# Ranking edges on one Trainium2 core: histogram matmuls written out at fixed places, and a quarter of the one-hot tiles made by ScalarE

## The chip, the cores and the metric

The kernel runs on one core of one Trainium2 chip, as one launch. The metric is device time in microseconds (us), the median of the runs shown. A core has TensorE (PE in the profile; its weight loads are PEld), VectorE (DVE), ScalarE (ACT), GpSimd (POOL) and SyncE (SP), which only issues transfers. A "q" behind an engine's name is its sequencer.

## What is computed

The reference is a four-layer graph network on 3125 nodes with 256 features and 50000 edges. Each layer adds a graph part, a linear-attention part and a feed-forward or expert part to x. The graph parts gather by `src` and sum by `dst` (or the reverse), for instance in layer 1:

```
s = einsum('edh,edh->eh', q[row], k[col])
m = segment_max(s, row);  e = exp(s - m[row])
attn = e / segment_sum(e, row)[row]
out = segment_sum(attn[:, None, :] * v[col], row)
```

To do such sums tile by tile the kernel first sorts the edges. Nothing else of the reference matters here: the change touches only the sorting.

## The kernel before

The first stage, `rank_edges`, computes for each edge the place that it takes in a table sorted by its key, in two orders: order 0 by `dst`, order 1 by `src`. The 50000 edges lie in a [128, ET] layout with ET = 400 columns, of 125 partitions in use. A key is split into a high part (`hi_f`, which of NT = 25 blocks of 128 nodes) and a low part (`lo_f`, 0 to 127). A column of 128 edges is called a tile. The constants are SU = 16 tiles in a group and SB = 8 tiles in a batch, so an order has 25 groups and 50 batches.

In an order:

- VectorE (lines 239 to 242) casts and splits the keys and signals `cast`. TensorE transposes them (lines 365 and 366), ScalarE copies the rows out (lines 439 and 440), SyncE stores them in HBM and reads them back as broadcasts for each batch (line 227).
- VectorE then loops over the 25 groups. Line 246 makes the one-hot rows of the high parts of 16 tiles at once (`hot_hi`, 16x25 columns), line 249 makes those of the low parts (`hot_lo`), 16 instructions of 128x128 bf16, one for each tile. Each group raises `hot` by two.
- TensorE loops over the same groups (line 370). For each tile it waits for `hot`, loads `hot_lo` as weights and multiplies `hot_hi` (line 373), adding up a 128x25 histogram in PSUM. The place of each tile is computed from the loop's counter in registers. Line 376 closes the sum and raises `histogram`.
- Meanwhile VectorE fills the records that will be scattered (lines 253 to 261) and does the first comparisons of the first batch (lines 280 and 274). Line 274 needs ScalarE's first distance (line 447), eight Abs over the broadcast keys.
- VectorE waits for `histogram`, copies it (line 285), and a short chain between VectorE and TensorE (lines 287 to 304, 379, 380, 395, 425) makes the places at which the buckets begin.
- The ranking loop goes over the 50 batches: TensorE counts (lines 386 and 395) and chooses (lines 406 and 408), ScalarE copies (line 454) and takes distances (line 447), VectorE compares (lines 268 and 274), selects (lines 314 to 318) and, after each second batch, writes the addresses of 16 tiles (line 334), which raises `placed`.

GpSimd waits for the records of order 0, and then for `placed` of order 0 before each 16 tiles; it scatters each tile's records into a table in HBM by an indirect transfer (line 482, 400 of them). It does nothing for order 1 in this stage: those records are scattered in layer 1, beside other work. Order 1 starts on VectorE when order 0's addresses are all written. The stage ends when all engines are through, the scatters have landed and the stage's 53 semaphores are cleared; then `prepare` reads the sorted table back (line 522).

The same way of making a one-hot tile on ScalarE that the change uses stands in the edge stages of the layers: eight Abs of iota minus the low part, then one Relu of one minus that over all eight (lines 657 and 661, and 1568 and 1572).

Of the kernel before, what the change touches and what calls it, by code (L numbers as in the profile page):

```python
# [22 lines left out]
ACT = mybir.ActivationFunctionType  # L23
# [3 lines left out]
ds = bass.ds  # L27
# [3 lines left out]
NT = -(-N // P)  # L31
# [7 lines left out]
SU = 16  # L39
ET = -(-E // (125 * SU)) * SU  # L40
# [80 lines left out]
    return ap.unsqueeze(at).to_broadcast(shape)  # L121


def rank_edges(kit, name, orders, room):

    nc, dram = kit.nc, kit.dram
    assert EFULL * ET == E and ET % SU == 0 and SU == 2 * SB
    chunks = [(c, min(P, ET - c)) for c in range(0, ET, P)]
    BATCHES = ET // SB
    with Stage(kit, name) as s:  # L130
# [7 lines left out]
        lo_f = s.sb("lo_f", [P, ET])  # L138
        etype = s.sb("etype", [P, ET], I32)
        spill = s.sb("spill", [P, ET])  # L140
        hot_lo = s.sb("hot_lo", [P, ET, P], BF16)
        hot_hi = flat_xn.bitcast(BF16)[:, 0:ET * NT].rearrange("p (t b) -> p t b", t=ET)
# [36 lines left out]
        cast, hot, histogram, totals, prefix, based, begins = ({} for _ in range(7))  # L179
        rowed, rows_copied, rows_stored, distanced, equalled, spread = ({} for _ in range(6))  # L180
        counted, high, split, chosen, selected, placed, recorded = ({} for _ in range(7))
        for o in range(2):
            for at_, what in ((cast, "cast"), (hot, "hot"), (histogram, "histogram"), (totals, "totals"),
                              (prefix, "prefix"), (based, "based"), (begins, "begins"), (rowed, "rowed"),
                              (rows_copied, "rows_copied"), (rows_stored, "rows_stored"), (distanced, "distanced"),
                              (equalled, "equalled"), (spread, "spread"), (counted, "counted"), (high, "high"),
                              (split, "split"), (chosen, "chosen"), (selected, "selected"), (placed, "placed"),
                              (recorded, "recorded")):
                at_[o] = s.sem(f"{what}{o}")
# [9 lines left out]
        with nc.Block() as block:  # L199
# [33 lines left out]
            def _(dve):  # L233
# [3 lines left out]
                def order(o, q):  # L237
# [7 lines left out]
                    with dve.Fori(0, ET // SU) as i:  # L245
                        v.tensor_tensor(hot_hi[:, ds(i * SU, SU), :], bcast(hi_f[:, ds(i * SU, SU)], NT, 2),
                                        bcast(kit.iota[:, 0:NT], SU, 1), ALU.is_equal).then_inc(hot[o], 1)
                        for u in range(SU):
                            ins = v.tensor_scalar(hot_lo[:, ds(i * SU + u, 1), :].squeeze(1), iota_b[:],
                                                  lo_f[:, ds(i * SU + u, 1)], None, ALU.is_equal)  # L250
                        ins.then_inc(hot[o], 1)
# [108 lines left out]
            def _(pe):  # L360
                def order(o):
# [5 lines left out]
                    ins.then_inc(rowed[o], 1)  # L367

                    nc.tensor.matmul(ps_run[:, 0:NT], zero_b[:], zero_b[:, 0:NT], start=True, stop=True)
                    with pe.Fori(0, ET // SU) as i:  # L370
                        for u in range(SU):
                            pe.wait_ge(hot[o], i * 2 + 2)
                            nc.tensor.matmul(ps_run[:, 0:NT], hot_lo[:, ds(i * SU + u, 1), :].squeeze(1),
                                             hot_hi[:, ds(i * SU + u, 1), :].squeeze(1), start=False, stop=True,
                                             skip_group_check=True)
                    nc.tensor.matmul(ps_run[:, 0:NT], zero_b[:], zero_b[:, 0:NT], start=False, stop=True,
                                     skip_group_check=True).then_inc(histogram[o], 1)
                    pe.wait_ge(totals[o], 1)
# [53 lines left out]
            @block.scalar  # L432
            def _(act):
                def order(o):
                    act.wait_ge(rowed[o], 1)
                    if o:
                        act.wait_ge(rows_stored[0], 2 * 16 * len(chunks))
                    for j, (c, w) in enumerate(chunks):
                        nc.scalar.copy(key_row[0:w, j, :], ps_row[0:w, 0, j, :]).then_inc(rows_copied[o], 1)
                        nc.scalar.copy(lo_row[0:w, j, :], ps_row[0:w, 1, j, :]).then_inc(rows_copied[o], 1)  # L440

                    def distance(n, u):

                        act.wait_ge(lined[o][u], (n - u) * 16 + 32)
                        act.wait_ge(chosen[o], n + 1)
                        for k in range(SB):
                            ins = nc.scalar.activation(apart[:, u, k, :], key_line[:, u, k * P:(k + 1) * P], ACT.Abs,
                                                       scale=-1.0, bias=key_f[:, ds(n * SB + k, 1)])
                        ins.then_inc(distanced[o], 1)

                    def turn(n, u, more):
                        act.wait_ge(counted[o], n + 1)
                        act.wait_ge(chosen[o], n + 1)
                        nc.scalar.copy(parts[:, u, 0].rearrange("p k b -> p (k b)"),
                                       ps_count[:, u, 0:(SB + 1) * NT]).then_inc(high[o], 1)
                        if more:
                            distance(n + 1, 1 - u)

                    distance(0, 0)
                    pairs(act, turn)  # L460

                order(0)
                order(1)

            @block.gpsimd
# [3229 lines left out]
```

## Time and profile before

| what | value |
|---|---|
| median of 3 runs | 7550.93 us (7548.48 to 7556.42) |
| the profiled execution, its own time | 7552.14 us |
| its span, first to last instruction | 7550.2 us |
| TensorE busy | 5770.7 us (76%), 22573 matmuls |
| VectorE busy | 4088.7 us (54%) |
| ScalarE busy | 2739.3 us (36%) |
| GpSimd busy | 3202.7 us (42%) |
| mean granted TensorE clock | 0.838 |

Busy times are sums over the whole span; the ranking stage is its first tenth (0 to 722.9 us), so shares over the span say little of it. All times of the timeline count from the span's start. In a timeline a row gives start, length, engine, line, operation, output and input, and in brackets the idle time of the engine before it with what ended it. "x16" means that 16 instructions are merged in the row; its length goes from the first's start to the last's end, and neighbours overlap.

### The profile page before, as it was taken

The numbers are of one execution on the slowest core, as the hardware profiler recorded it, in microseconds if no ns is written. First come the engines' busy times: TensorE is split into PE (matmuls) and PEld (weight loads), VectorE is DVE, ScalarE is ACT, GpSimd is POOL, SyncE is SP. The second block draws the span as 40 slices with busy tenths as digits, with TensorE's granted clock in tenths as the row PEclk, the third lists the DMA queues.
The fourth block names the chain that finished last, engine by engine and source line by source line (L and its number), as shares of the span: only waits on it lengthen the run. The fifth ranks groups of instructions, "written<-read, shape, count | busy, mean of one in ns | idle before, by whom it ended". The sixth has DMA issues, their size and how long they took to land. (4 is left out here: it accounts for less than half of the span.)

```text
span 7550.2 us, 91454 instructions
## 1 busy us (share of the span) xinstructions
PE 5770.7 (76%) x22573; PEld 3591.7 (48%) x22664; DVE 4088.7 (54%) x9995; ACT 2739.3 (36%) x7575; POOL 3202.7 (42%) x3209
## 2 busy tenths in 40 slices
PE   5564688888985788876976787998788858998386
PEld 3332355554542565642545553554455535565253
DVE  7876577733113899966245334213577775556401
ACT  2524477721220444410114432113166615555010
POOL 1776576404772666610017750000177715553101
PEclk9999788888997778778988887898778766987597
DMA  2534222100001655510013330000144423333222
GB/s 87 165 86 155 50 50 47 31 12 28 2 2 53 172 158 157 159 32 13 0 60 105 105 75 23 0 0 14 47 117 115 112 58 105 98 98 69 76 99 74
DMA packets 268803, 549.15 MB, mean 73 GB/s; under 512 B 86992, under 2 KB 136588, under 8 KB 263692
## 3 DMA queue, kind: packets, MB, share of 16 engines
q0 software_dynamic: 134496, 314.63, 16.6%
q1 hardware_dynamic: 133932, 230.20, 9.5%
q8 instruction: 153, 2.51, 0.1%
q14 instruction: 222, 1.82, 0.1%
HBM read 495.56 MB, written 49.00 MB: 72 GB/s over the span
## 5 line engine op out<-in xcount | busy, mean ns | idle before, releaser
L1252 POOL DMA_INDIRECT L_edges_rows<-scratch_L_kv,L_edges_index x416 | 496.8, 1194 | 379.7 <-PE L_edges_ps_sum L1501 213.0
L1252 POOL DMA_INDIRECT L3a_edges_rows<-scratch_L3a,L3a_edges_index x416 | 462.5, 1112 | 409.5 <-DMA L3a_edges_last<-order_dst_last 257.1
L1252 POOL DMA_INDIRECT L3b_edges_rows<-scratch_L3b,L3b_edges_index x416 | 398.6, 958 | 400.8 <-PE L3b_edges_ps_sum L1501 236.3
L1702 POOL TENSOR_TENSOR L_norm_fold<-L_norm_square 128x400 f32<-128x400 f32 x64 | 66.6, 1040 | 1168.3 <-ACT L_norm_square L1711 1168.3
L482 POOL DMA_INDIRECT scratch_by_dst<-dst_record,dst_dest x400 | 439.7, 1099 | 271.1 <-DVE dst_dest L334 149.5
L1252 POOL DMA_INDIRECT L_edges_rows<-scratch_L,L_edges_index x416 | 424.4, 1020 | 257.3 <-issue 117.8
L632 POOL DMA_INDIRECT L_edges_rows<-scratch_L,L_edges_index x416 | 396.8, 954 | 274.5 <-SPq L616 148.0
L2324 DVE TENSOR_TENSOR L_experts_gated_h<-L_experts_hidden,L_experts_ps_g 128x800 f32<-128x800 f32 x112 | 110.6, 988 | 665.0 <-PE L_experts_ps_g L2277 665.0
L482 POOL DMA_INDIRECT scratch_by_src<-src_record,src_dest x400 | 383.1, 958 | 124.0 <-issue 121.7
L2315 ACT ACTIVATE L_experts_hidden<-L_experts_ps_h,L_eb_sb 128x400 f32<-128x400 f32 x320 | 190.2, 594 | 646.2 <-PE L_experts_ps_h L2270 646.2
L1373 DVE TENSOR_TENSOR L_acc<-L_edges_ps_sum,L_acc 128x264 f32 (+1 forms) x832 | 357.0, 429 | 98.5 <-DVE L_acc L1373 70.2
L644 PE MATMUL L_edges_ps_sum<-L_edges_rows,L_edges_hot 128*128 128x256 f32 x832 | 259.2, 476 | 143.8 <-issue 91.9
L684 DVE TENSOR_TENSOR L_acc<-L_edges_ps_sum,L_acc 128x256 f32 x416 | 176.7, 425 | 282.2 <-PE L_edges_ps_sum L644 248.2
L1501 PE MATMUL L3b_edges_ps_sum<-L3b_edges_rows,L3b_edges_hot 128*128 128x258 f32 x832 | 322.4, 536 | 4.2 <-DVE L_acc L1373 4.2
L2270 PE MATMUL L_experts_ps_h<-xn,L_e_sb 128*128 128x400 f32 x896 | 323.3, 504 | 2.6 <-PEq L113 2.6
L2287 PE MATMUL L_experts_ps_o<-L_experts_gated_h,L_e_sb 128*128 128x400 f32 x896 | 322.0, 499 | 2.2 <-DVE L_experts_gated_h L2324 2.2
L1501 PE MATMUL L_edges_ps_sum<-L_edges_rows,L_edges_hot 128*128 128x272 f32 x832 | 307.9, 503 | 6.1 <-DVE L_edges_rows L1355 6.1
L1568 ACT ACTIVATE L_edges_hot<-iota,L_edges_lo 128x128 f32<-128x128 f32 x832 | 252.8, 386 | 150.1 <-DMA L_edges_last<-order_src_last 92.8
L1604 ACT ACTIVATE L_edges_rhs<-L_edges_msg,L_edges_rhs 128x64 f32<-128x64 f32 x1248 | 303.6, 334 | 1.7
L1446 PE MATMUL L_edges_ps_key<-L_q,L_edges_hot_t 128*128 x832 | 270.5, 483 | 42.6 <-ACT L_edges_asked L1579 26.7
L1501 PE MATMUL L_edges_ps_sum<-L_edges_rhs,L_edges_hot 128*128 128x264 f32 x832 | 298.2, 491 | 0.0
L1501 PE MATMUL L3a_edges_ps_sum<-L3a_edges_rows,L3a_edges_hot 128*128 128x264 f32 x832 | 296.1, 488 | 0.6 <-issue 0.4
(767 smaller groups left out, 13541.3 us busy)
## 6 DMA issues: line engine op xcount, KB each, us to landing
x<-scratch_dst_key_rows SPq DMA_DIRECT2D x50, 512.0 KB, 4.7
x<-scratch_src_key_rows SPq DMA_DIRECT2D x50, 512.0 KB
L_experts_w<-in_L_w SPq DMA_DIRECT2D x16, 1024.0 KB
L_edges_rows<-scratch_L,L_edges_index POOLq DMA_INDIRECT x832
L_edges_lo_rows<-order_src_lo_rows SPq DMA_DIRECT2D x52, 256.0 KB
L3a_edges_lo_rows<-order_dst_lo_rows SPq DMA_DIRECT2D x52, 256.0 KB
L3b_edges_lo_rows<-order_dst_lo_rows SPq DMA_DIRECT2D x52, 256.0 KB
x<-scratch_dst_lo_rows SPq DMA_DIRECT2D x50, 256.0 KB, 3.7
```

The lines of the kernel that those rows point to most:

```text
L482: pool.indirect_dma_start(order["table"], bass.IndirectOffsetOnAxis(order["dest"][:, t:t + 1], 0), order["record"][:, t, :], None).then_in ...
L632: pool.indirect_dma_start(rows[:, n % RING, k, :], None, row_table, bass.IndirectOffsetOnAxis(index[:, t:t + 1].bitcast(U32), 0)).then_inc ...
L644: nc.tensor.matmul(ps_sum[:, k % 4, 0:F], hot[:, n % RING, k, :], rows[:, n % RING, k, :], start=True, stop=True).then_inc(summed, 1)
L1252: pool.indirect_dma_start(rows[:, n % RING, k, 0:RW], None, row_table, bass.IndirectOffsetOnAxis(index[:, t:t + 1].bitcast(U32), 0)).then_ ...
L1373: v.tensor_tensor(a, ps_sum[:, (c * SB + k) % BANKS, 0:M], a, ALU.add).then_inc(merged, 1)
L1446: ins = nc.tensor.matmul(ps_key[:, j % 2, (k % 2) * D:(k % 2 + 1) * D], hot_t[:, c % 2, k * P:(k + 1) * P], key_rows[:, ds(r[k], 1), :].sq ...
L1501: nc.tensor.matmul(ps_sum[:, (c * SB + k) % BANKS, 0:M], hot[:, c % RING, k, :], values(c)[:, k, :], start=True, stop=True).then_inc(summe ...
L1568: ins = nc.scalar.activation(hot[:, c % RING, k, :], kit.iota[:], ACT.Abs, scale=-1.0, bias=lo[:, ds(n * SB + k, 1)])
L1604: ins = nc.scalar.activation(out, src, ACT.Copy, scale=parts(c)[:, k, h, V:V + 1])
L2270: ins = nc.tensor.matmul(ps_h[:, (a + o) % 4, 0:CW], weights[l][:, e, f, o * P:(o + 1) * P], r, start=f == 0, stop=f == len(src) - 1)
L2287: nc.tensor.matmul(ps_o[:, o, 0:CW], weights[hid][:, e, f, o * P:(o + 1) * P], gated_h[:, n % 2, f, :], start=e == 0 and f == 0, stop=False)
L2315: nc.scalar.activation(hidden[l][:, n % 2, o, :], ps_h[:, a % 4, 0:CW], func, bias=biases[l][:, n % EX, o:o + 1]).then_inc(taken, 1)
```

## The change

Two edits, in both orders. VectorE's inner loop makes 12 of a group's 16 `hot_lo` tiles; ScalarE makes the last 4, between its copies of the rows and its first distance: four Abs of iota minus the low part into the tile's place, a wait for itself (`hot_apart`), and one Relu over the four tiles in place, which raises `hot_act`. In order 1 ScalarE first waits until TensorE has done all 50 counts of order 0, the last reads of the old tiles. TensorE's loop over groups is written out in the program: each tile has a fixed place, there is one wait for `hot` per group, and one for `hot_act` before the thirteenth tile. Four semaphores are new.

```diff
+ACT_TILES = 4
...
                     with dve.Fori(0, ET // SU) as i:
...
-                        for u in range(SU):
+                        for u in range(SU - ACT_TILES):
                             ins = v.tensor_scalar(hot_lo[:, ds(i * SU + u, 1), :].squeeze(1), iota_b[:],
                                                   lo_f[:, ds(i * SU + u, 1)], None, ALU.is_equal)
                         ins.then_inc(hot[o], 1)
...
-                    with pe.Fori(0, ET // SU) as i:
+                    for i in range(ET // SU):
+                        pe.wait_ge(hot[o], i * 2 + 2)
                         for u in range(SU):
-                            pe.wait_ge(hot[o], i * 2 + 2)
-                            nc.tensor.matmul(ps_run[:, 0:NT], hot_lo[:, ds(i * SU + u, 1), :].squeeze(1),
-                                             hot_hi[:, ds(i * SU + u, 1), :].squeeze(1), start=False, stop=True,
-                                             skip_group_check=True)
+                            if u == SU - ACT_TILES:
+                                pe.wait_ge(hot_act[o], i + 1)
+                            nc.tensor.matmul(ps_run[:, 0:NT], hot_lo[:, i * SU + u, :], hot_hi[:, i * SU + u, :],
+                                             start=False, stop=True, skip_group_check=True)
...
+                    act.wait_ge(cast[o], 1)
+                    if o:
+                        act.wait_ge(counted[0], BATCHES)
+                    for i in range(ET // SU):
+                        for u in range(SU - ACT_TILES, SU):
+                            ins = nc.scalar.activation(hot_lo[:, ds(i * SU + u, 1), :].squeeze(1), kit.iota[:], ACT.Abs,
+                                                       scale=-1.0, bias=lo_f[:, ds(i * SU + u, 1)])
+                        ins.then_inc(hot_apart[o], 1)
+                        act.wait_ge(hot_apart[o], i + 1)
+                        here = hot_lo[:, ds(i * SU + SU - ACT_TILES, ACT_TILES), :]
+                        nc.scalar.activation(here, here, ACT.Relu, scale=-1.0, bias=kit.ones[:, 0:1]).then_inc(hot_act[o], 1)
```

## Rows read from the trace of the kernel before

**Rows 1.** Stretches: us, busy (count) of PE, PEld, DVE, ACT, POOL, clock, DMA share, GB/s

```profile
19.00:103.50 84.50, 54.36 (x298) 31.57 (x298) 79.47 (x425) 3.80 (x16) 0.00 (x0) 1.00 0.12 39
...
475.50:700.30 224.80, 127.21 (x1306) 84.85 (x1306) 192.60 (x461) 137.01 (x442) 176.32 (x160) 1.00 0.56 168
```

**Rows 2.** Line 482, GpSimd's scatters: durations min/median/max, first and last start; what its idle time ended on

```profile
L482 POOL DMA_INDIRECT scratch_by_dst<-dst_record,dst_dest x400: 954/958/1992, 149.9 to 710.3; - x134
...
  DVE dst_dest L334: 149.5, 1
```

**Rows 3.** Timeline at the end of the ranking stage

```profile
700.06 0.18 DVE L334 TENSOR_TENSOR src_dest<-x,rank_spill 128x16 uint32<-128x16 f32 x1
...
710.33 0.95 POOL L482 DMA_INDIRECT scratch_by_dst<-dst_record,dst_dest  x1 [0.30 <-issue]
722.88 0.32 SPq L522 DMA_DIRECT2D prepare_dst_rec<-scratch_by_dst  x1
```

**Rows 4.** Timeline of order 0, from the histogram's groups to the ranking

```profile
26.47 0.57 DVE L246 TENSOR_TENSOR xn<-rank_hi_f,iota 128x400 f32 x1 [0.19 <-issue]
...
26.96 2.69 DVE L249 TENSOR_SCALAR rank_hot_lo<-rank_iota_b,rank_lo_f 128x128 bf16 x16
...
100.25 0.58 DVE L246 TENSOR_TENSOR xn<-rank_hi_f,iota 128x400 f32 x1 [0.17 <-issue]
...
110.05 1.22 DVE L274 SCALAR_TENSOR_TENSOR rank_apart<-rank_apart,rank_later_b 128x1024 bf16<-128x1024 bf16 x1
110.17 0.32 SPq L227 DMA_DIRECT2D x<-scratch_dst_lo_rows  x1
...
134.35 0.18 DVE L285 COPY rank_total<-rank_ps_run 128x25 f32<-128x25 f32 x1 [23.08 <-PE rank_ps_run L376]
...
142.36 2.44 ACT L447 ACTIVATE rank_apart<-x,rank_key_f 128x128 bf16<-128x128 f32 x8 [0.29 <-PE rank_ps_pick L408]
```

**Rows 5.** Timeline, TensorE, one group of the histogram in order 0

```profile
76.48 3.92 PE L373 MATMUL rank_ps_run<-xn,rank_hot_lo 128*128 x16 [0.54 <-issue]
```

**Rows 6.** Line 373: the register operations of TensorE's sequencer

```profile
L373 PEldq FUSED_REGOPS  x800: 74/74/89, 22.5 to 474.8; - x160
L373 PEldq ALU_OP  x800: 32/32/42, 22.7 to 474.9; - x160
```

**Rows 7.** Timeline, the first and the last of 16 choosing matmuls

```profile
141.49 0.21 PE L406 MATMUL rank_ps_pick<-rank_ones_b,rank_apart 128*128 128x1 bf16 x1
...
142.02 0.20 PE L408 MATMUL rank_ps_pick<-rank_parts,xn 128*128 128x50 bf16 x1
```

**Rows 8.** Groups by line, 19 to 104 us: busy us, mean ns, idle before

```profile
L249 DVE TENSOR_SCALAR rank_hot_lo<-rank_iota_b,rank_lo_f 128x128 bf16 x400 | 67.2, 249 | 0.0
```

**Rows 9.** Timeline, ScalarE: the last copy of rows, and eight Abs in layer 2

```profile
22.17 0.25 ACT L440 CAST rank_lo_row<-rank_ps_row 16x128 bf16<-16x128 f32 x1
...
3943.62 2.43 ACT L657 ACTIVATE L_edges_hot<-iota,L_edges_lo 128x128 f32<-128x128 f32 x8
```

**Rows 10.** Groups by line, ScalarE, whole span

```profile
L1568 ACT ACTIVATE L_edges_hot<-iota,L_edges_lo 128x128 f32<-128x128 f32 x832 | 252.8, 386 | 150.1 <-DMA L_edges_last<-order_src_last 92.8 <-DMA L_edges_dirs<-order_dst_dirs 57.3
...
L1572 ACT ACTIVATE L_edges_hot<-L_edges_hot,ones 128x1024 f32<-128x1024 f32 x104 | 119.4, 1148 | 3.4
...
L1713 ACT ACT_TABLE_LOAD x8 | 10.3, 1283 | 0.1
```

**Rows 11.** Transfers up to 160 us: issues, KB each, median us to landing

```profile
x<-scratch_dst_key_rows SPq DMA_DIRECT2D x8, 512.0 KB, 5.5
```

**Rows 12.** Timeline, order 1: VectorE's wait for the histogram

```profile
475.49 0.18 DVE L285 COPY rank_total<-rank_ps_run 128x25 f32<-128x25 f32 x1 [31.70 <-PE rank_ps_run L376]
```

**Rows 13.** Granted clock: mean of the core; then one stretch, columns as in rows 1

```profile
core 0: 7550.2 us, clock 0.838
...
7050.00:7144.00 94.00, 51.63 (x193) 37.49 (x192) 40.48 (x103) 7.93 (x10) 6.22 (x6) 0.57 0.19 77
```

**Rows 14.** Stretch from the histogram's copy to the first scatter, columns as in rows 1

```profile
134.35:149.90 15.55, 10.34 (x77) 6.51 (x78) 10.72 (x33) 7.84 (x26) 0.00 (x0) 1.00 0.34 103
```

More of the change, by code:

```diff
@@ L181, in rank_edges @@
         counted, high, split, chosen, selected, placed, recorded = ({} for _ in range(7))
+        hot_apart, hot_act = {}, {}
         for o in range(2):
-            for at_, what in ((cast, "cast"), (hot, "hot"), (histogram, "histogram"), (totals, "totals"),
+            for at_, what in ((cast, "cast"), (hot, "hot"), (hot_apart, "hot_apart"), (hot_act, "hot_act"), (histogram, "histogram"), (totals, "totals"),
                               (prefix, "prefix"), (based, "based"), (begins, "begins"), (rowed, "rowed"),
```

## The prediction

> **What bounds the kernel now.** Only the ranking stage changes, so I first cut it into stretches. While order 0 makes its one-hot tiles (19 to 103.5 us) VectorE is busy 79.5 of 84.5 us and GpSimd does nothing; in the ranking of order 1 all the engines work [rows 1]. Next: what does GpSimd, which scatters the records, wait for? For another engine just once, 149.5 us, until the first addresses (line 334) are there. From 149.9 us its 400 scatters follow each other to 710.3 us, 1.40 us apart on average [rows 2]. The end of the stage shows who sets it: VectorE has written the last addresses of order 1 at 700.2 us, GpSimd ends its last scatter at 711.3, and the next stage starts at 722.9 [rows 3]. So the stage's end is "first scatter + 400 scatters + 11.6 us", and VectorE's own end lies 11 us before it. A scatter takes 1.405 us of wall time beside the ranking loop (160 in 224.8 us) and 0.95 + 0.30 = 1.25 where the other engines rest [rows 1, 3]. What counts is how early the first address comes, in order 0.
>
> That is set in the histogram. In order 0 VectorE turns out a group of 16 tiles every 3.354 us (26.47 to 100.25 is 22 groups), ends the records and the first comparison (line 274) at 110.05 + 1.22 = 111.3, and then idles 23.1 us until 134.35, for TensorE's last histogram matmul [rows 4]. TensorE needs 3.92 us for 16 matmuls and 0.54 between groups, 4.46 together [rows 5]. Beside each matmul its sequencer does two register operations, of 74 and 32 ns [rows 6]. From 134.35 to the first scatter at 149.9 runs a chain of 15.55 us that the change leaves alone.
>
> **Part 1, matmuls written out.** It removes 400 pairs of register operations per order, 400 waits (one per group stays, and one more for ScalarE's tiles) and the turn of the loop. The pitch is now 3.92/16 = 0.245 us. Upper bound for the new one: 0.245 less the 0.106 of register work is 0.139, so 16 x 0.139 + 0.54 = 2.76 us a group. Lower bound: in the ranking the matmuls of lines 406 and 408, each with a stationary load of 128x128 bf16 as here, start 16 times between 141.49 and 142.02, 0.035 us apart; that is 0.6 us a group [rows 7]. I take the lower one and 0.2 for the wait, since engine, type and tile are the same: 0.8 us. Even at the upper bound TensorE is through with 25 groups at 22.8 + 25 x 2.76 = 92 us, and VectorE needs it at 95 (below). It is no longer what ends last.
>
> **Part 2, VectorE makes 12 tiles in place of 16.** Its 16 tiles run 2.69 us and one lasts 0.249, so the pitch is (2.69 - 0.249)/15 = 0.163 us [rows 4, 8]. Four fewer in 25 groups are 100 x 0.163 = 16.3 us. At the full 0.249 it would be 24.9. A gain of nothing is excluded by the room between the tiles: 16 of them fill 2.69 of the 3.354 us. The group falls to 2.70 us.
>
> **Part 3, ScalarE makes 4.** Each group adds four Abs, a wait of the engine for its own result, and one Relu over 512 columns. Later stages have the same idiom with 8 tiles: eight Abs in 2.43 us, one of them 0.386, so the pitch is 0.292; then 3.4/104 = 0.03 us of idle; then a Relu over 1024 columns in 1.148 [rows 9, 10]. Over 512 columns, by (1.148 - 0.386)/896 = 0.85 ns a column, it takes 0.71. A group is 3 x 0.292 + 0.386 + 0.03 + 0.71 = 2.01 us; half of the idiom with 8 tiles would be 1.8, and a ceiling is four unlapped Abs with the whole Relu, 2.7. ScalarE is free when its copies end, at 22.17 + 0.25 [rows 9]. 25 groups end at 22.4 + 50 = 73 us (ceiling 90). Queued behind them is the first distance, eight Abs of 2.43 us, for which VectorE asks at about 93.8: ready at 75 (ceiling 92.5), so nobody waits. Until then ScalarE has no other work. In order 1 it first waits until order 0's counts are done, which they are before VectorE starts that order.
>
> **Part 4, what is late next.** VectorE's line 274 ends at 111.3 - 16.3 = 95.0, the histogram 1 to 2 us after VectorE's last tile (87.1), and line 285 starts at 95.1 in place of 134.35: 39.2 us earlier. The broadcasts of the third batch, released by VectorE's first comparison (110.17, then 93.9), are asked for by ScalarE at 142.36, then 103.1 [rows 4]. The cover shrinks from 32 to 9.2 us; such a broadcast lands in 5.5 us [rows 11], so it costs nothing. SP's queue gets no new entry. Four more semaphores are cleared at the stage's end; all 53 of now take no more than the 11.6 us there, so four take at most 0.9, and I take 0.
>
> **Order 1** saves the same 16.3 us and the 31.7 us for which VectorE waits there [rows 12]. It is worth nothing: the scatters cover it, and that cover grows from 11 to some 59 us. Without it, it would be worth up to 48.
>
> **The sum.** First scatter 149.9 - 39.2 = 110.7, next stage at 683.7, all the rest moved as a whole. The profiled execution took 7552.14 us (span 7550.2), 1.2 above the median of the runs: 7552.1 - 39.2 = 7512.9, or 7512 against the median. With 24.9 in place of 16.3 it would be 7503.
>
> **A rule against it.** The trace grants TensorE the full clock through the ranking of order 1, though it is busy only 127 of 225 us [rows 1]; late in the kernel, with 51.6 of 94 us busy, it grants 0.57 [rows 13]. The new histogram is thinner than both, some 0.8 in each 2.7 us. At half the clock a group of 16 would take 1.4 us, still inside 2.7; but the chain of 15.55 us holds 10.3 us of TensorE records [rows 14], and doubling all of them would cost at most 10.3: 7522. I take nothing for it [rows 1] and keep 7522 in the range. The Trainium skill's page "TensorE: Matmul & The Clock Gate" (Part 1) has it that an array which idles falls back to 1.2 GHz and gets 2.4 again only when busy. By that rule the 7522 would be the result.
>
> **The rivals.**
> (a) Registers don't make the pitch of 0.245; only the loop's turn goes. TensorE then keeps about 3.95 us a group and ends at 22.8 + 98.8 = 121.6, 12.6 us earlier than now: 7538. Against it: the pitch of 0.035 us [rows 7]. Chance 0.05.
> (b) Slower: later stages meet a lower clock. The mean granted clock is 0.838 [rows 13], with TensorE busy 5771 us (the table above); if all of that lay on the path, a mean below 0.832 would eat the 39 us, and 0.830 would cost 5771 x (0.838/0.830 - 1) = 56, net 16 slower: 7567. For it: late stretches are granted little more than half. Against it: those stages do the same work, only sooner, and three runs lie within 8 us. Chance 0.04.
> (c) Abs and Relu change tables. Two loads of 1.283 us a group make it 2.01 + 2.57 = 4.58 us; ScalarE ends at 137, its distance after one more load at 140.6, line 285 at 142: 8 us slower, 7558. Against it: 104 Relus right behind Abs had 3.4 us of idle before them in all [rows 10]. Chance 0.02.
> (d) VectorE's chain, not the scatters, ends the stage; both savings count: 39.2 + 47.9 = 87, 7464. Against it: one wait, and the order of the ends [rows 2, 3]. Chance 0.02.
> (e) The edit is there, but ScalarE comes late by 25 us or more and takes most of it back. Within 0.2%. Chance 0.02.
>
> **How the numbers follow.** The forecast, 7512, has 0.85. 0.2% is 15 us, about what a measurement of this kernel can tell from no change. Faster are the forecast, (d) and a little of (a): 0.88. Within 0.2%: most of (a), (c) and (e), 0.08. Slower: (b), 0.04. The range goes from 7502 (the bound with 24.9) to 7526 (half the clock in the chain, and the 4 us by which runs differ).
>
> **What would show it.** Right: VectorE's groups 2.70 us apart; line 285 at 95 us with no wait for TensorE; 16 matmuls in about 0.8 us, TensorE idle between groups for VectorE; ScalarE's groups 2.0 us apart, done near 73; first scatter near 111, last near 671; order 1's addresses done near 613, and GpSimd alone for 59 us after. Wrong: a wait before line 285 or 274, a ScalarE group over 2.9 us, a granted clock below 1 before 120 us, scatters slower than 1.40 on average, or later stages of another length.

## The result and the profile after

The changed kernel takes 7498.52 us (median of 4 runs, 7492.41 to 7505.47) against 7549.70 for the kernel before (4 runs, 7536.44 to 7556.42): ratio 0.9934, 95% interval 0.9919 to 0.9949. That is 51 us faster than these 4 runs. From the 7550.93 us that was known when the prediction was made it is 52 us, where the forecast of 7512 meant 39 and the range allowed 49. A later comparison on another chip gave 0.9935 [0.9920, 0.9951]. The profiled execution took 7501.76 us, with a span of 7500.0, which is 50.2 below the span of before.

Lines after the edits have moved: 246, 249, 274, 285 and 334 of before are 250, 253, 278, 289 and 338 now; 373 is 379, 447 is 464, 482 is 499 and 522 is 539. ScalarE's new tiles are lines 452 (Abs) and 457 (Relu).

First the timeline of the new kernel, rows of four engines out of order 0 [rows 4, 5, 9].

```profile
22.89 1.27 ACT L452 ACTIVATE rank_hot_lo<-iota,rank_lo_f 128x128 bf16<-128x128 f32 x4
24.19 0.72 ACT L457 ACTIVATE rank_hot_lo<-rank_hot_lo,ones 128x512 bf16<-128x512 bf16 x1
24.82 1.26 ACT L452 ACTIVATE rank_hot_lo<-iota,rank_lo_f 128x128 bf16<-128x128 f32 x4
...
77.17 0.58 DVE L250 TENSOR_TENSOR xn<-rank_hi_f,iota 128x400 f32 x1
77.27 0.61 PE L379 MATMUL rank_ps_run<-xn,rank_hot_lo 128*128 128x25 bf16 x16 [1.88 <-DVE rank_hot_lo L253]
77.66 2.04 DVE L253 TENSOR_SCALAR rank_hot_lo<-rank_iota_b,rank_lo_f 128x128 bf16 x12
79.66 0.58 DVE L250 TENSOR_TENSOR xn<-rank_hi_f,iota 128x400 f32 x1
...
82.80 2.73 DVE L257 MEMSET dst_record<- 128x3200 int32 x1 [0.61 <-issue]
88.80 1.22 DVE L278 SCALAR_TENSOR_TENSOR rank_apart<-rank_apart,rank_later_b 128x1024 bf16<-128x1024 bf16 x1
89.94 0.18 DVE L289 COPY rank_total<-rank_ps_run 128x25 f32<-128x25 f32 x1
93.64 0.35 ACT L471 CAST rank_parts<-rank_ps_count 128x225 bf16<-128x225 f32 x1 [20.27 <-PE rank_ps_count L400]
```

TensorE does its 16 matmuls in 0.61 us and then waits 1.88 for VectorE. VectorE starts a group every 2.49 us (77.17 to 79.66) with no idle time ahead of it; before it was 3.354, with 0.17 to 0.19 idle. A ScalarE group takes 1.93 us (22.89 to 24.82), and ScalarE has 20 us to spare before its next copy. Line 289 follows the first comparison with no wait in between: the 23.08 us are gone.

Second, by line: the copy of the histogram (both orders), the scatters and the last addresses [rows 2, 3, 12], then the scatters' releaser. "First and last start" are the last two times of a row.

```profile
L289 DVE COPY rank_total<-rank_ps_run x2: 178/178/178, 89.9 to 382.8; 128x25 f32<-128x25 f32 x2
...
L499 POOL DMA_INDIRECT scratch_by_dst<-dst_record,dst_dest x400: 954/958/1992, 105.5 to 666.8; - x134
...
  DVE dst_dest L338: 105.0, 1
...
L338 DVE TENSOR_TENSOR src_dest<-x,rank_spill x25: 174/175/176, 397.8 to 607.3; - x24, 128x16 uint32<-128x16 f32 x1
```

And the end of the stage in the timeline [rows 3], with the stretch of order 0's histogram (columns as in rows 1).

```profile
666.77 0.96 POOL L499 DMA_INDIRECT scratch_by_dst<-dst_record,dst_dest  x1 [0.30 <-issue]
679.35 0.32 SPq L539 DMA_DIRECT2D prepare_dst_rec<-scratch_by_dst  x1
...
19.00:82.70 63.70, 17.52 (x410) 14.35 (x410) 62.78 (x326) 50.93 (x141) 0.00 (x0) 1.00 0.16 52
```

| event | before | after | difference |
|---|---|---|---|
| histogram's copy, order 0 | 134.4 | 89.9 | -44.4 |
| first scatter | 149.9 | 105.5 | -44.4 |
| histogram's copy, order 1 | 475.5 | 382.8 | -92.7 |
| last addresses of order 1 | 700.1 | 607.3 | -92.8 |
| last scatter | 710.3 | 666.8 | -43.5 |
| next stage's first read | 722.9 | 679.35 | -43.5 |
| end of span | 7550.2 | 7500.0 | -50.2 |

Order 1 gained 48 us more than order 0, and the end of the stage shows none of it: GpSimd scatters for 60 us after the last addresses are there. A further 6.7 us (50.2 - 43.5) appear in later stages, whose source the change leaves alone.

### The profile page after: what moved, and what is told of

It is laid out like the page before. It is cut to its first block and busy times, and to the rows that moved or that the text cites. A ratio compares the mean times of both kernels' runs of the same rounds, so it can differ in the third digit from the quotient of the medians.

```text
span 7500.0 us, 89553 instructions
## 1 busy us (share of the span) xinstructions
PE 5662.0 (75%) x22573; PEld 3530.3 (47%) x22664; DVE 4055.7 (54%) x9795; ACT 2832.1 (38%) x7825; POOL 3208.0 (43%) x3209
```

## The experiments

A difference "at line 289" below is always to the 134.4 us of the kernel before (line 285 there, or the line that answers to it). Every ratio is to runs of the kernel before on the same chip.

### One order or one half of the change, on a chip that stands still

**order0_only**: the change in order 0, the old loops in order 1. **order1_only**: the other way round.

```diff
-                        for u in range(SU - ACT_TILES):
+                        for u in range(SU - (ACT_TILES if o == 0 else 0)):
...
+                    if o == 0:
                         for i in range(ET // SU):
                             pe.wait_ge(hot[o], i * 2 + 2)
...
+                    else:
+                        with pe.Fori(0, ET // SU) as i:
```

> The change in order 0 alone; order 1 as before. Theory (the first address of order 0 sets the stage's end, the scatters cover order 1): first scatter at 105.5 us as with the full change, prepare starts 43.5 us earlier than before, the whole gain of the full change is there: about 0.9935 of before. VectorE waits about 31 us for TensorE in order 1 and nobody pays. Rival (order 1's saving counts too): less than the full gain, the time lies 6 to 8 us or more over that of the full change, and prepare starts later than with it.

> The change in order 1 alone; order 0 as before. Theory (scatters cover order 1): first scatter stays at 150 us, VectorE's last addresses come about 48 us earlier (652), GpSimd's last scatter stays at 710, time within 0.2% of before. Rival (order 1's saving counts): 7 us or more faster than before, the prepare stage starting earlier than 722.9. A third thing read here: VectorE's group of 16 tiles in order 0 lasted 3.354 us before against 3.12 in order 1; if that is a matter of the place of the code or of the order, it stays 3.35 here.

**written_out_only**: TensorE's matmuls written out, VectorE makes all 16 tiles. **act_tiles_only**: ScalarE makes 4 tiles, TensorE keeps its loop with computed places.

```diff
-ACT_TILES = 4
+ACT_TILES = 0
...
-                    for i in range(ET // SU):
-                        for u in range(SU - ACT_TILES, SU):
...
```

(With 0 tiles ScalarE's whole new block is left out too.)

```diff
-                    for i in range(ET // SU):
-                        pe.wait_ge(hot[o], i * 2 + 2)
+                    with pe.Fori(0, ET // SU) as i:
                         for u in range(SU):
-                            if u == SU - ACT_TILES:
+                            pe.wait_ge(hot[o], i * 2 + 2)
+                            if u >= SU - ACT_TILES:
```

> Only the matmuls written out (0 of 16 tiles on ScalarE). Theory (register work and the wait for each tile made TensorE slow): TensorE's 16 matmuls take about 0.6 us and it waits for VectorE; line 285 of before starts right behind the first comparison, at 111 us, 23 us earlier; stage end 23 us earlier, about 7527, 0.997 of before. Rival (the pitch of 0.245 us is of the matmuls with their loads): 16 matmuls still take 3.9 us, gain 12 us or less. On VectorE: if the 0.17 us of idle in front of each group of order 0 came from TensorE's polling for each tile, the group falls from 3.35 to 3.14 and the gain grows to 28 us; if not, it stays 3.35.

> Only ScalarE's four tiles; TensorE's loop with registers as before, plus waits for ScalarE's tiles. Theory (TensorE was the bound of the histogram): its group stays 4.46 us or grows by the added waits' register work (some 0.03 to 0.1 us for each of four tiles), VectorE's group is 2.5 us and VectorE then idles 39 us or more; time as before or up to 10 us slower. Rival (VectorE's tiles were the bound, or both alternate): 16 us or more faster.

These four ran on a chip on which the kernel before took 8730.68 us, not 7550:

| kernel | median us | ratio [95%] | line 289 |
|---|---|---|---|
| order0_only | 8685.06 | 0.9940 [0.9921, 0.9959] | -44.6 |
| order1_only | 8694.26 | 0.9942 [0.9920, 0.9964] | +0.2 |
| written_out_only | 8662.40 | 0.9911 [0.9892, 0.9929] | -23.1 |
| act_tiles_only | 8739.21 | 1.0010 [0.9996, 1.0024] | +10.3 |

At line 289 the parts can be read all the same, since order 0's histogram was undisturbed. With the whole change in order 0 alone it came 44.6 us earlier, as with the change. Written out alone, it came 23 us earlier: the wait for TensorE goes, and VectorE's own 3.35 us a group sets the time. ScalarE's tiles alone made it later by 10, because TensorE was the bound and each of the four added waits inside its loop slowed it further. The timeline of act_tiles_only shows one group of TensorE and VectorE's wait:

```profile
61.66 2.94 PE L379 MATMUL rank_ps_run<-xn,rank_hot_lo 128*128 x12 [0.58 <-issue]
64.75 0.18 PE L379 MATMUL rank_ps_run<-xn,rank_hot_lo 128*128 x1 [0.15 <-issue]
65.10 0.18 PE L379 MATMUL rank_ps_run<-xn,rank_hot_lo 128*128 x1 [0.17 <-DVE xn L250]
...
144.66 0.18 DVE L289 COPY rank_total<-rank_ps_run 128x25 f32<-128x25 f32 x1 [54.91 <-PE rank_ps_run L382]
```

Twelve matmuls take 2.94 us, 0.245 each, and those behind a wait of their own are 0.35 apart. The two halves don't add: -23 and +10 against -44.4 together. Only with TensorE out of the way does a lighter VectorE pay.

The totals, though, went against my forecast that order 1 is worth nothing: order1_only gained 36 us here. Why is in the records of order0_only: one row of VectorE's timeline and the scatters' releasers.

```profile
278.03 0.57 DVE L318 TENSOR_TENSOR x<-rank_ps_pick,xn 128x400 f32<-128x400 f32 x1 [36.84 <-remote]
...
L508 POOL DMA_INDIRECT scratch_by_dst<-dst_record,dst_dest x400: 952/958/1892, 105.3 to 725.9; - x134
...
  DVE dst_dest L338: 203.1, 10
```

The ranking loop stood still for up to 36.84 us at a time on something that the profile calls remote, and GpSimd waited for addresses ten times, 203 us in all (105 of them for the first, as ever). The last addresses of order 1 came at 1058.8 us, long after the last scatter at 725.9, and the next stage started at 1060.3. With VectorE's chain so late, the scatters no longer set the stage's end and both orders' savings count, as in my rival (d). The sizes don't add up there: the written-out kernel gained 68 us, where 23.1 for order 0 and 31.7 for order 1 make 55. The traces of all four kernels show the standing still. The kernel before has no trace from that chip, only its time. What the loop stood still on stays open. The question of order 1 had to be asked again elsewhere.

### The same question on an undisturbed chip

**order1_again** and **written_out_again** are the kernels of above, here beside 14 runs of the kernel before (7542.76 us).

> The change in order 1 alone once more. On the chip of the first four runs the ranking loops stood still for up to 37 us at a time, so that order 1 ended long after the scatters; on a chip without that the scatters should cover it. Theory: first scatter 150 us, last 710, prepare starts at 723, within 0.2% of before. Rival (order 1's saving counts even so): 7 us or more faster, prepare starting before 716. If the standing still shows again (last addresses of order 1 after 1000 us), the saving of some 48 us counts in full.

> Only the matmuls written out, both orders, once more, for a chip without the standing still. Theory: first scatter at 126.8 us (23.1 earlier), prepare at 700, 23 us faster than before, 0.9969; order 1 saves 31.7 us, which is covered. Where the ranking loops stand still, the two savings add up, 55 us.

order1_again: 7548.54 us, ratio 1.0000 [0.9990, 1.0011]. By line:

```profile
L289 DVE COPY rank_total<-rank_ps_run x2: 176/181/186, 134.9 to 427.7; 128x25 f32<-128x25 f32 x2
...
L338 DVE TENSOR_TENSOR src_dest<-x,rank_spill x25: 174/175/177, 442.7 to 651.9; - x24, 128x16 uint32<-128x16 f32 x1
...
L508 POOL DMA_INDIRECT scratch_by_dst<-dst_record,dst_dest x400: 954/958/1970, 150.5 to 710.2; - x134
```

Order 1's histogram is copied 47.8 us earlier (427.7 against 475.5), its last addresses come 48.2 earlier, and the last scatter starts at 710.2 in place of 710.3. The forecast's 47.9 us are there to within 0.3, and the scatters cover all of them. So this part of the argument is shown.

written_out_again: 7516.77 us, 0.9956 [0.9937, 0.9975]. Line 289 comes 22.3 us earlier and the next stage 21.0. The timeline has both engines:

```profile
74.18 0.61 PE L379 MATMUL rank_ps_run<-xn,rank_hot_lo 128*128 128x25 bf16 x16 [2.74 <-DVE rank_hot_lo L253]
...
94.41 0.57 DVE L250 TENSOR_TENSOR xn<-rank_hi_f,iota 128x400 f32 x1 [0.18 <-issue]
94.91 2.69 DVE L253 TENSOR_SCALAR rank_hot_lo<-rank_iota_b,rank_lo_f 128x128 bf16 x16
97.77 0.58 DVE L250 TENSOR_TENSOR xn<-rank_hi_f,iota 128x400 f32 x1 [0.18 <-issue]
```

TensorE's 16 matmuls take the same 0.61 us as in the changed kernel, and VectorE's group is still 3.36 us with its 0.18 idle. So of the 44.4 us, 22.3 are TensorE's and 22.1 are the four tiles: 0.88 us a group, where my pitch gave 0.65.

### Where VectorE's missing 0.22 us a group comes from

**three_tiles**, **five_tiles**: another number of ScalarE's tiles. **after_again**: the change, again. **written_out_padded**: nine more clears of a small tile on VectorE ahead of the ranking loops, which only move the code behind them.

```diff
-ACT_TILES = 4
+ACT_TILES = 5
```

```diff
+                for _ in range(9):
+                    link(v.memset(zeros[:], 0.0))
```

> The change with 3 of 16 tiles on ScalarE, 13 on VectorE. It tells what the extra 0.22 us of a group of 16 tiles in order 0 is (3.354 us there, 3.12 in order 1; 12 tiles 2.487, 11 tiles 2.325 in both). Theory A (a step that only the long loop body at its place has): 13 tiles take 2.487 + 0.163 = 2.65 us in both orders. Theory B (a tile costs 0.217 throughout in order 0): 2.70 in order 0. Theory C (the step comes between 12 and 13 tiles): 2.87 in order 0.

> As the change, with 5 of 16 tiles on ScalarE. Theory: VectorE's group falls by one tile pitch, 0.163 us, to 2.32 us; ScalarE's grows from 1.92 to 2.32 (0.29 for the Abs, 0.11 for 128 more columns of the Relu), still not behind. First scatter at 101.5 us, 4 us before that of the change; time 4 us less than the change, 0.9929 of before. Rival (a tile costs VectorE 0.217 us a group, as 16 against 12 tiles showed): group 2.27, first scatter at 100.1. Rival (ScalarE becomes the bound): TensorE ends after VectorE's first comparison, no gain or a loss against the change.

> The change itself once more, beside the next kernel on the same chip. Theory (only the ranking stage changes, what comes after differs from run to run): first scatter 105.5 us, prepare starts 43.5 us earlier, and the median gain lies at 44 us, about 0.9942 of before; the 51 of the first comparison held some 7 us of the later stages' scatter. Rival (the change also speeds the later stages): a gain of 50 us or more again, 0.9935 or less.

> Only the matmuls written out, with nine small memsets and their waits put ahead of everything in VectorE's first wait, so that its loops lie some 18 instructions further on. Theory A1 (the place of the loop's code makes the 0.22 us): the group of 16 tiles changes in order 0 or in order 1, 3.354 to 3.13 or the other way. Theory A2 (it is the order itself, such as GpSimd at work beside order 1, or traffic): 3.354 in order 0 and 3.13 in order 1 as ever.

| kernel | VectorE's tiles | us a group, order 0 | order 1 | median us | ratio [95%] |
|---|---|---|---|---|---|
| before | 16 | 3.37 | 3.13 | 7550.93 | |
| written_out_padded | 16 | 3.37 | 3.38 | 7519.03 (one run) | |
| three_tiles | 13 | 2.65 | 2.66 | 7498.43 (one run) | |
| after_again | 12 | 2.49 | 2.49 | 7500.91 | 0.9935 [0.9920, 0.9951] |
| five_tiles | 11 | 2.32 | 2.32 | 7494.57 | 0.9931 [0.9910, 0.9952] |

(Means over the 24 intervals from the first group to the last. The first interval is longer than the others in some kernels: order 0 of before has 3.79 us there and 3.354 behind it.) Each tile is worth some 0.163 us, as forecast, from 11 tiles to 13 and from there to 3.13 with 16. What doesn't fit is 3.37 alone, which before shows in order 0 and not in order 1, though both orders run the same instructions. This is order 1 of before, with 3.09 and no idle time between two groups:

```profile
366.78 0.56 DVE L246 TENSOR_TENSOR xn<-rank_hi_f,iota 128x400 f32 x1
367.26 2.68 DVE L249 TENSOR_SCALAR rank_hot_lo<-rank_iota_b,rank_lo_f 128x128 bf16 x16
369.87 0.57 DVE L246 TENSOR_TENSOR xn<-rank_hi_f,iota 128x400 f32 x1
```

Nine clears ahead of the loops made order 1 slow too. This was no longer a matter of how many tiles, but of where the loop's code lies; so four more kernels asked that directly. (Below, "the dear place" is short for a place of the code at which the loop takes the longer time.)

**before_padded** and **after_padded**: the nine clears in the kernel before and in the changed one. **before_padded_4**: four clears. **one_wait**: the kernel before with TensorE's wait told once per group, loop and computed places kept.

```diff
                     with pe.Fori(0, ET // SU) as i:
+                        pe.wait_ge(hot[o], i * 2 + 2)
                         for u in range(SU):
-                            pe.wait_ge(hot[o], i * 2 + 2)
```

> The kernel before with 9 more clears of the zero tile on VectorE ahead of the ranking loops (under 10 us even if each took 1.2 us, off the path of order 0's loop only if TensorE is the bound there, so line 285 may move later by a few us). Place of the code: the stages after the ranking stage, whose source is the same, take another time than the 6827 us that the kernel before spends after prepare's start (6826.6 with order 1 alone changed), by 5 to 15 us, as the padding shifts VectorE's later instructions. Rival, the later stages gain from something that the change of the ranking stage leaves behind (an earlier start against work of other queues): then the rest stays at 6827 within 2 us, since the ranking stage is not changed.

> The change with the same 9 clears. Place of the code: the time after prepare's start leaves 6820.7 to 6822.6 us (the change's two profiles) by 5 us or more, towards 6812.8 (what the padded written-out kernel showed); VectorE's 12-tile group stays at 2.49 us, since its body is shorter. Rival: the rest stays at 6821 within 2 us.

> The kernel before with 4 clears instead of 9. Place of the code: the time after prepare's start differs from that with 9 clears and from 6827 by several us; an effect of the clears themselves, not of the place, would give the same as with 9 to within 1 us.

> The kernel before with TensorE's wait told once per group instead of before each of the 16 matmuls, loop and computed places kept. If the waits inside the group cost as much as the places computed in registers, TensorE's 16 matmuls fall from 3.92 to about 2.3 us, VectorE's 3.35 us becomes the bound, and line 285 starts 22 us earlier, as with the matmuls written out (-22.3). If the registers are nearly all of it, 16 matmuls stay at 3.4 us or more and line 285 starts 0 to 13 us earlier.

| kernel | order 0 | order 1 | line 289 | next stage | span | median us | ratio [95%] |
|---|---|---|---|---|---|---|---|
| before_padded | 3.37 | 3.38 | +0.1 | -0.3 | 7553.4 | 7557.55 | 1.0012 [1.0002, 1.0021] |
| before_padded_4 | 3.37 | 3.38 | +1.0 | +4.5 | 7546.3 | 7548.08 (one run) | |
| after_padded | 2.70 | 2.49 | -40.6 | -42.5 | 7484.6 | 7500.10 | 0.9939 [0.9922, 0.9955] |
| one_wait | 3.37 | 3.13 | +0.5 | -0.1 | 7559.7 | 7561.65 (one run) | |

The timeline of after_padded has order 0 and order 1 with the same 12 tiles:

```profile
27.03 0.57 DVE L250 TENSOR_TENSOR xn<-rank_hi_f,iota 128x400 f32 x1 [0.16 <-issue]
27.52 2.04 DVE L253 TENSOR_SCALAR rank_hot_lo<-rank_iota_b,rank_lo_f 128x128 bf16 x12
29.71 0.58 DVE L250 TENSOR_TENSOR xn<-rank_hi_f,iota 128x400 f32 x1 [0.15 <-issue]
...
322.20 0.57 DVE L250 TENSOR_TENSOR xn<-rank_hi_f,iota 128x400 f32 x1
322.69 2.20 DVE L253 TENSOR_SCALAR rank_hot_lo<-rank_iota_b,rank_lo_f 128x128 bf16 x12
324.70 0.56 DVE L250 TENSOR_TENSOR xn<-rank_hi_f,iota 128x400 f32 x1
```

The first loop has 2.68 us between group starts and 0.15 to 0.16 idle (2.70 as a mean), the second 2.50 with none. I had expected the 12 tiles to stay at 2.49 in both orders; in order 0 they did not. Counted over both orders, this is the idle time ahead of a group's first instruction (columns: us, times), in before, before_padded and after_padded:

```profile
L246 DVE TENSOR_TENSOR xn<-rank_hi_f,iota x50: 558/575/589, 19.3 to 435.6; 128x400 f32 x50
...
  issue: 4.6, 24
```

```profile
L246 DVE TENSOR_TENSOR xn<-rank_hi_f,iota x50: 574/576/637, 19.2 to 442.0; 128x400 f32 x50
...
  issue: 6.3, 35
```

```profile
L250 DVE TENSOR_TENSOR xn<-rank_hi_f,iota x50: 559/574/586, 18.5 to 379.4; 128x400 f32 x50
...
  issue: 4.0, 24
```

24 is every turn of order 0, in all three. The 35 of before_padded are these and 11 of order 1. The other turns of its order 1 take as long without an idle time in the record:

```profile
371.26 0.57 DVE L246 TENSOR_TENSOR xn<-rank_hi_f,iota 128x400 f32 x1
...
374.63 0.58 DVE L246 TENSOR_TENSOR xn<-rank_hi_f,iota 128x400 f32 x1
```

So the idle time is a sign of the dear place, and the distance between group starts is the measure. In the changed kernel this line has no idle on issue at all. The 0.22 us are shown to depend on where the loop's code lies: the same 12 tiles take 2.49 or 2.70 us, and the same 16 take 3.13 or 3.38. The change takes four tiles out of the body, each with the register operation that the trace shows beside it, and this got order 0's loop out of the dear place; nothing in the prediction had foreseen it. The cases fit one picture: a boundary in the code that costs 0.2 us when a loop runs across it, and that in order 0 lies behind the end of a body of 13 tiles and before that of one of 16. That picture is an inference; no run moved the code step by step.

In the expectations for these kernels I had asked that later stages move as well, by 5 us or more. Single profiles show movements, without pattern: from the next stage's first read to the end before_padded took 6830.8 us (7553.4 - 722.6), before_padded_4 6818.9, one_wait 6836.9 and before 6827.3 (before_padded thus moved by 3.5, less than asked). after_padded took 6804.2 and the changed kernel 6820.7. But after_padded's profiled execution was the fastest of its four (7486.75 to 7518.21), and the others are single profiles. The medians give a little more. Nine clears that change line 289 and the next stage by 0.3 us at most made the kernel before 6 us slower (ratio 1.0012, its interval just above 1). That hints that something behind the ranking stage moves by some microseconds when nothing but the place of the code changes; it does not show it.

one_wait settles TensorE's loop. A timeline row, with the register operations of its sequencer:

```profile
76.98 3.92 PE L373 MATMUL rank_ps_run<-xn,rank_hot_lo 128*128 x16 [0.53 <-issue]
...
L373 PEldq FUSED_REGOPS  x800: 74/74/89, 23.0 to 475.2; - x160
L373 PEldq ALU_OP  x800: 32/32/42, 23.2 to 475.3; - x160
```

With 15 of 16 waits gone a group still takes 3.92 us. The waits were free; what costs is the place computed in registers, 0.245 us a matmul against some 0.03 written out (15 intervals in 0.61 - 0.18 us). The two recorded register operations are 0.106 us of that difference of 0.21. The rest has no record.

### A version that beats both

**five_tiles_early_zero**, and again as **best_again** on another chip: five tiles by ScalarE, and the clear of the records (2.73 us in order 0) moved ahead of the loops, where VectorE waits for its input anyway.

```diff
-ACT_TILES = 4
+ACT_TILES = 5
...
-                    link(v.memset(record, 0))
...
+                for q in orders:
+                    link(v.memset(q["record"], 0))
```

> As five tiles, and the zeroing of the two record tables (2.7 us before order 0's records, 1.4 before order 1's) is moved into VectorE's first wait for the inputs, 6.3 us long. Theory: first scatter 2.7 + 0.6 us earlier than with five tiles alone, at 98.3 us; time 7 us below the change, 0.9925 of before. Rival (something else then ends last before the histogram's copy, such as ScalarE's first distance or the histogram itself): less than 2 us of that shows.

> Five tiles on ScalarE and the record tables zeroed in VectorE's first wait, once more. Theory: first scatter at 100.3 us, prepare starts 49.5 us earlier, 6 us below the change run on the same chip: about 0.9934 of before if the change is 0.9942. Rival: the 6 us are lost behind the scatters, no difference from the change.

Medians 7483.48 us, ratio 0.9922 [0.9900, 0.9943], and 7484.69, ratio 0.9914 [0.9897, 0.9932]. On the latter chip the changed kernel took 7500.91, so this is 16 us less. With five tiles VectorE and ScalarE need 2.32 us each (five_tiles, timeline):

```profile
31.56 0.83 ACT L457 ACTIVATE rank_hot_lo<-rank_hot_lo,ones 128x640 bf16<-128x640 bf16 x1
31.67 0.58 DVE L250 TENSOR_TENSOR xn<-rank_hi_f,iota 128x400 f32 x1
32.29 1.55 ACT L452 ACTIVATE rank_hot_lo<-iota,rank_lo_f 128x128 bf16<-128x128 f32 x5
...
33.88 0.83 ACT L457 ACTIVATE rank_hot_lo<-rank_hot_lo,ones 128x640 bf16<-128x640 bf16 x1
33.99 0.58 DVE L250 TENSOR_TENSOR xn<-rank_hi_f,iota 128x400 f32 x1
```

With the clear moved too, ScalarE becomes what is late, in five_tiles_early_zero:

```profile
81.08 2.42 ACT L465 ACTIVATE rank_apart<-x,rank_key_f 128x128 bf16<-128x128 f32 x8
...
83.54 1.23 DVE L277 SCALAR_TENSOR_TENSOR rank_apart<-rank_apart,rank_later_b 128x1024 bf16<-128x1024 bf16 x1 [2.10 <-ACT rank_apart L465]
```

So moving the clear made line 289 just 1.1 to 1.6 us earlier than five tiles alone (84.7 and 85.2 against 86.3), where I had expected 3.3 for the first scatter. The next stage came 46.6 us earlier with five tiles and 49.6 and 46.8 us with the clear moved (the changed kernel: 43.5 and 44.8). That is 2 to 6 us of the 16. The other 10 or more lie in later stages again (6805.2 and 6806.5 us from the next stage to the end, against 6820.7 and 6822.6 of the changed kernel). They were there both times; their cause was not found.

The record shows what they go with. The mean granted clock is 0.841 to 0.846 in the nine runs of this version, 0.8436 on average, and 0.834 to 0.842 in the ten runs of the changed kernel, 0.8389 on average. Among the 38 runs of the kernel before on the three chips where it took 7550 us, a run with a clock higher by 0.001 was shorter by some 3.4 us (a line fitted to them, correlation -0.6). By that line, an estimate, 0.0047 would go with 16 us. Which of the two is the cause, and why this version has the higher clock, is not shown.

## Why the prediction was wrong in size and right in mechanism

What held, step by step:

- **The frame.** "First scatter + 400 scatters + 11.6": the scatters from first to last start took 561.3 us against 560.4, 0.9 of the gain lost to a pitch of 1.407 in place of 1.405 (in after_again they took 560.0, so this differs from one execution to the next), and the end of the stage is 12.6 us after the last start, as before. The four semaphores cost nothing that shows.
- **Part 1.** 0.8 us a group was forecast for TensorE, 0.61 measured. The pitch of lines 406 and 408 [rows 7] was the right neighbour to take. The upper bound of 2.76 credited only the recorded register operations; one_wait and the written-out kernels show that twice as much hung on the computed places. Rival (a) is out.
- **Part 3.** 2.01 us a group for ScalarE was forecast, 1.93 measured; no table load, so rival (c) is out, and VectorE and TensorE did not wait for it (e).
- **Order 1.** Forecast 47.9 us and covered; measured 48.3 (92.7 less 44.4), and covered (order1_again: ratio 1.0000). Rival (d) did not happen, except on the chip where the ranking loop stood still.
- **The clock.** The stretch of order 0 has TensorE busy 17.5 of 63.7 us and the granted clock at 1.00, the full 2.4 GHz. The 7522 that I had kept for half the clock in the chain did not come, nor rival (b): the mean granted clock is 0.838, as before. By the rule of the Trainium skill's page "TensorE: Matmul & The Clock Gate" (Part 1) an array that idles falls back to 1.2 GHz; this stage, with 1.88 us of waiting in each 2.49, does not show it.

**What failed is the term of Part 2**: "100 x 0.163 = 16.3 us". The pitch of 0.163 was right (12 tiles run 2.04 us: (2.04 - 0.249)/11 = 0.163). What I kept constant was the rest of the group, 3.354 less 16 tiles. It held an idle time of 0.17 to 0.19 us on issue at each turn of the loop. That was in my own row [rows 4], in brackets, and I took it for part of the loop. Order 1 of before ran the same loop in 3.13 us without it; from there I would have had 2.48 as a second value for the new group. The steady groups of order 0 went from 3.354 to 2.49 us, 0.21 more than the four tiles, and the first turn of before had a further gap of 0.4. Together that is 24 x 0.21 + 0.4 = 5.5 us: 16.3 became 21.8. Line 285 then moved by

| term | forecast | measured |
|---|---|---|
| wait for TensorE gone | 23.1 | 23.1 |
| four tiles less in 25 groups | 16.3 | 16.3 |
| loop out of the dear place, 24 turns of 0.21 | 0 | 5.1 |
| gap in the first turn | 0 | 0.4 |
| input landed later (line 250 first starts at 19.9, not 19.3) | 0 | -0.6 |
| whole, by line 285 | 39.2 | 44.4 |

(0.1 to 0.2 of rounding and overlap are left in both columns.) after_padded shows the forecast's world: with its loop in the dear place a steady group takes 2.69 us, as good as the forecast's 2.70. Its line 289 comes 3.8 us later than in the changed kernel although its first group starts 1.4 us earlier (18.5 for 19.9), so the place costs 5.1 us there.

**The second step that failed is "all the rest moved as a whole",** which put the change of the later stages at nothing. They took 6.7 us less in the one profile, and 4.7 in the other (6827.3 against 6822.6). By the medians 51.2 - 43.5 leaves 8; for after_again 46.8 - 44.8 leaves 2, though its ratio of 0.9935 is that of the rival in its expectation and not the 0.9942 that I expected. A higher granted clock does not go with it: the ten runs of the changed kernel average 0.839, the 38 of the kernel before 0.841. Starting points of later stages show where it goes in the profiled pair: nothing yet at 1805 us (-43.2), then -48.7 by 3239 us, -53.4 at 4508, and -50.2 at the end. before_padded, whose ranking stage ends as in before, wanders along the same points by -6.9, -10.8, -8.1 and +3.2. So movements of this size come with nothing but nine clears added ahead of the ranking loops. Whether it is the place of the code there too, as in the ranking loop, was not tried, and the cause stays open; one kernel's own runs lie up to 30 us apart (7532.97 to 7562.92 in 13 runs of before), and separating 5 us by stage would take many profiles of each. That the whole gain lies in the ranking stage is therefore not shown; 43.5 to 44.8 us of it do.

In sum, of the 13 us between 7512 and the measured 7498.5 some 4 are the loop's place (5.2 at line 285, less the 0.9 of the scatters), 7 the later stages of the profiled pair, and 2 that the profiled executions lie differently far above their medians (3.2 us now, 1.2 before). The range of 7502 to 7526 missed by 3.5 us since both misses had the same sign and its lower end allowed for just one: the full duration of a tile (24.9 for 16.3), a bound on the wrong quantity.

## What to carry to other kernels

Before costing "n instructions fewer in a loop" as n times their pitch, look at what the loop's turn costs in each place where the same loop runs: idle time on issue ahead of the body's first instruction that one copy has and another doesn't is a cost of place, and an edit of the body can remove it or bring it. Places computed in registers can cost a stream of small matmuls far more than the register operations' own records (0.21 us here for 0.106 recorded); writing them out pays where that engine is the bound, and moving work to an idle engine pays only after that. And count a saving only as far as the engine that sets the stage's end: 48 us in order 1 were worth nothing here, and would be worth their full size when that end moves to another engine.

## What the runs showed of the hardware that was not expected

- The place of the code changes a small loop on VectorE by 0.21 to 0.25 us a turn: 2.49 or 2.70 us with 12 tiles, 3.13 or 3.38 with 16. The Trainium skill's page "Runtime: NRT & Kernel Launch" (Instruction fetch mechanics) says that instructions are fetched in blocks of 256 and that a branch out of the two blocks at hand stalls; our loop's body has 34 recorded instructions with 16 tiles (line 246 and the tiles, 17 in all, and a register operation beside each), so a crossing of one boundary would keep within two blocks. No run here shows what the boundary is.
- Waits whose semaphore is already there cost TensorE nothing in a loop of 16 matmuls (one_wait, 3.92 us with 1 or 16), but a second wait with a computed value made it 0.35 us a matmul for 0.245.
- On one of the chips the ranking loops stood still for up to 38.1 us at a time and the kernel before took 8730.68 us, 16% more. The ranking stage is the smaller part of it: against order1_again, order1_only spent 333 us more up to the next stage's first read and 817 us more behind it, at a mean granted clock of 0.812 in place of 0.841. Ratios on it (0.9940 and 0.9942 for one order each) answer another question than those elsewhere (1.0000 for order 1): compare the kernel before's own time across chips before reading a ratio.
